# Twelve-stage transformer kernel: where PE fillers stand, how value projections are interleaved, and the order of three row gathers

## Time and profile before

| | |
|---|---|
| Three runs | 518.43, 514.8, 518.2 us |
| Median | 518.2 us |
| Profiled execution | 517.47 us, its span 515.7 us |
| PE busy | 471.1 us (91% of the span) |
| DVE busy | 330.1 us (64%) |
| ACT busy | 239.2 us (46%) |
| POOL busy | 66.7 us (13%) |
| Mean granted PE clock | 0.977 |

### The profile page before, as it was taken

How to read it: one execution, slowest core, us unless ns; L and a number is a source line. 1 busy time by engine, 2 the same in 40 slices (tenths; PEclk the granted TensorE clock), 3 DMA queues, 4 the chain that set the end, 5 groups by cost and what they waited for, 6 DMA issues and landing times.

```text
span 515.7 us, 10193 instructions
## 1 busy us (share of the span) xinstructions
PE 471.1 (91%) x4120; PEld 388.0 (75%) x4120; DVE 330.1 (64%) x815; ACT 239.2 (46%) x480; POOL 66.7 (13%) x149
## 2 busy tenths in 40 slices
PE   8988999999875869899989899889999999999897
PEld 6857885555664868656557779769899899999797
DVE  5666579984745836898335464376777777755644
ACT  7223546777400434666733246275566565532131
POOL 1220124000016020200014005500000000001000
PEclk9989999999898898999999999899999999999999
DMA  7908301910177734000019000000000000019000
GB/s 261 396 3 175 74 1 41 208 22 1 30 282 255 291 93 159 1 1 0 2 60 390 3 1 1 2 0 1 1 0 2 1 1 1 1 42 417 34 1 5
DMA packets 9070, 42.05 MB, mean 82 GB/s; under 512 B 2287, under 2 KB 4919, under 8 KB 6327
## 3 DMA queue, kind: packets, MB, share of 16 engines
q1 hardware_dynamic: 7297, 32.73, 19.5%
q0 software_dynamic: 1728, 8.68, 4.6%
HBM read 34.72 MB, written 0.08 MB: 67 GB/s over the span
## 4 chain that ended last, share of the span: by engine, by line
PE 61%; DVE 18%; DMA 7%; issue 6%; POOL 4%; ACT 3%; SPq 1%; POOLq 0%; DVEq 0%; ACTq 0%
PE banks L281 55%; PE banks L284 6%; DVE peaks L1566 4%; DMA p_const<-in_const 3%; DMA region<-in_tree_v,leaf_no 2%; DMA region<-in_tree_f,leaf_no 1%; DVE probs L1563 1%; DVE small L2559 1%; POOL mv L386 1%; DVE probs L634 1%; DVE nmax L633 1%; DVE nmax L630 1%; DVE xnT L399 1%; ACT probs L655 1%; SPq L307 1%
## 5 line engine op out<-in xcount | busy, mean ns | idle before, releaser
L281 PE MATMUL banks<-identb 128*128 128x128 bf16 x944 | 69.2, 230 | 8.4 <-DMA region<-in_tree_q,leaf_no 3.9
L281 PEld LDWEIGHTS banks<-identb 128*128 128x128 bf16 x944 | 63.3, 104 | 11.4 <-DMA region<-in_tree_q,leaf_no 4.1
L1566 DVE TENSOR_REDUCE peaks<-banks 128x1 f32<-128x1024 f32 x56 | 66.5, 1220 | 4.2 <-PE banks L281 3.1
L2559 DVE TENSOR_REDUCE small<-banks 128x1 f32<-128x1024 f32 x32 | 39.1, 1222 | 24.3 <-PE banks L281 24.1
L2653 ACT CAST weights_hi<-banks 128x512 fp32r<-128x512 f32 x64 | 35.0, 590 | 27.4 <-PE banks L284 23.4
L284 PE MATMUL banks<-p_first,probs 128*128 128x128 f32 x320 | 44.2, 275 | 3.5 <-ACT probs L658 1.7
L2644 ACT ACTIVATE probs<-banks,nmax 128x1024 f32<-128x1024 f32 x32 | 35.6, 1115 | 24.5 <-DVE nmax L2563 24.4
L2569 DVE TENSOR_TENSOR weights_lo<-banks,weights_hi 128x512 fp32r<-128x512 f32 x64 | 41.4, 683 | 7.4 <-ACT weights_hi L2653 7.4
L284 PEld LDWEIGHTS banks<-p_first,probs 128*128 128x128 f32 x320 | 36.4, 140 | 10.6 <-ACT probs L655 2.3
L1650 ACT ACTIVATE region<-banks,seen 128x512 f32<-128x512 f32 x64 | 37.9, 702 | 12.2 <-PE banks L281 12.2
L1650 ACT ACTIVATE region<-banks 128x512 f32<-128x512 f32 x64 | 33.4, 606 | 17.1 <-PE banks L281 16.7
(11 more groups left out here) (493 smaller groups left out, 907.6 us busy)
## 6 DMA issues: line engine op xcount, KB each, us to landing
region<-in_w_l2f SPq DMA_DIRECT2D x1, 4096.0 KB, 15.4
region<-in_w_l3f SPq DMA_DIRECT2D x1, 4096.0 KB, 13.5
region<-in_w_b SPq DMA_DIRECT2D x1, 3076.0 KB, 14.7
values<-in_ctx SPq DMA_DIRECT2D x2, 1024.0 KB, 7.9
region<-in_w_l0f SPq DMA_DIRECT2D x1, 2048.0 KB, 21.7
keys_l1x<-shared SPq DMA_DIRECT2D x8, 256.0 KB, 4.1
keys_l2x<-probsT SPq DMA_DIRECT2D x8, 256.0 KB, 5.1
region<-in_w_l3d SPq DMA_DIRECT2D x1, 2048.0 KB, 17.0
```

Source lines behind the costliest of these rows:

```text
L281: return nc.tensor.matmul(o, lhsT, rhs, start=start, stop=stop)
L1566: nc.vector.tensor_reduce(peaks[:, h // 4 % 2, i:i + 1], ps[:, 2 * a:2 * a + 2, :], AX.XY, ALU.max, negate=True).then_inc(VM.sem, VM.now(( ...
L2559: return nc.vector.tensor_reduce(small[:, half:half + 1], ps[:, 2 * half:2 * half + 2, :], AX.XY, ALU.max)
```

## The change

It has three parts.

1. In l1x each value projection is split into two halves of two matmuls, and the eight places between peaks are filled anew: key 0 and half of value 0 behind peak 0, then half a value behind each of peaks 1 and 2, and so on. Only the second half signals.
2. In l2x PE waits, behind peak 9, for the maximum of peak 6, and issues 22 fillers into bank 4; behind turn(0) it issues 20 more.
3. In l1f the two first-layer halves of v are gathered ahead of k's second layer; DVE makes v's hidden units ahead of k's products; the row maximum of the attention scores moves into the chain of v, ahead of its fourth step; the fillers ahead of tree q are 76 instead of 44.

```diff
-                def value(b):
-                    if b == 2:
+                def value(b, half):
+                    if b == 2 and half == 0:
                         pe.wait_ge(A.sem, A.at(("l2x", "k", 0)))
-                    if b == 3:
+                    if b == 3 and half == 0:
                         pe.wait_ge(A.sem, A.at((tag, "v", 1)))
-                    for j in range(4):
+                    for j in (2 * half, 2 * half + 1):
                         t = 4 * b + j
                         m = mm(ps[:, VALUE_BANKS[b], j * P:(j + 1) * P], ctxT[:, t * P:(t + 1) * P], w("v"))
-                    m.then_inc(T.sem, T.now((tag, "vp", b)))
+                    if half:
+                        m.then_inc(T.sem, T.now((tag, "vp", b)))
...
-                early = {0: (key, 0), 1: (value, 0), 2: (value, 1), 3: (key, 1), 4: (key, 2), 5: (value, 2), 6: (key, 3),
-                         7: (value, 3)}
+                early = (((key, 0), (value, 0, 0)), ((value, 0, 1),), ((value, 1, 0),), ((value, 1, 1), (key, 1)),
+                         ((key, 2), (value, 2, 0)), ((value, 2, 1),), ((key, 3), (value, 3, 0)), ((value, 3, 1),))
...
                 if first:
                     peak(9)
+                    pe.wait_ge(VM.sem, VM.at((tag, 3, 0)))
+                    keep(22, 4)
                 if masked:
                     pe.wait_ge(A.sem, A.at((tag, "v", 3)))
                 turn(0)
-                if not first:
+                if first:
+                    keep(20, 4)
+                else:
                     peak(9)
...
             if n == "q":
                 loaded(pe, "leaf0_q")
-                keep(44, 0)
+                keep(76, 0)
...
-        def tree_chain(dve, n, base):
+        def tree_chain(dve, n, base, between=None):
             h = units(n)
             for j in range(CHAIN):
+                if j == 3 and between is not None:
+                    between()
...
-                for n in "qk":
-                    tree_hidden(dve, n, tA[:, :])
-                    tree_products(dve, n)
+                tree_hidden(dve, "q", tA[:, :])
+                tree_products(dve, "q")
+                tree_hidden(dve, "k", tA[:, :])
                 tree_hidden(dve, "v", tA[:, :])
-                dve.wait_ge(T.sem, T.at("l1f.s"))
-                vl(dve, nc.vector.tensor_reduce(s[:, 0:1], ps[:, 0, 0:P], AX.X, ALU.max))
-                nc.vector.tensor_scalar(s[:, 1:2], s[:, 0:1], -1.0 / np.sqrt(float(P)), None,
-                                        ALU.mult).then_inc(V.sem, V.now("l1f.m"))
+                tree_products(dve, "k")
+
+                def largest():
+                    dve.wait_ge(T.sem, T.at("l1f.s"))
+                    vl(dve, nc.vector.tensor_reduce(s[:, 0:1], ps[:, 0, 0:P], AX.X, ALU.max))
+                    nc.vector.tensor_scalar(s[:, 1:2], s[:, 0:1], -1.0 / np.sqrt(float(P)), None,
+                                            ALU.mult).then_inc(V.sem, V.now("l1f.m"))
+
                 loaded(dve, "leaf2_v")
-                tree_chain(dve, "v", tree_bias("v"))
+                tree_chain(dve, "v", tree_bias("v"), largest)
...
                 tree_gather_halves(pool, "k", "l1f.paths.even", "l1f.paths")
+                tree_gather_halves(pool, "v", "l1f.paths.even", "l1f.paths")
                 tree_gather(pool, "k", (2,))
-                tree_gather_halves(pool, "v", "l1f.paths.even", "l1f.paths")
                 tree_gather(pool, "v", (2,))
```

More of the change, by code:

```diff
@@ L1489, in _ @@
                     if masked and k < 8:
-                        step, b = early[k]
-                        step(b)
+                        for step, *which in early[k]:
+                            step(*which)
                 if first:
                     peak(9)
+                    pe.wait_ge(VM.sem, VM.at((tag, 3, 0)))
+                    keep(22, 4)
                 if masked:
@@ L1736, in build, with tree_plan @@
         PRODUCTS = {"q": 2, "k": 2}
-        def tree_plan(n, func=False):
+        def tree_plan(n, func=False, first=None):
             if func:
@@ L1746, in tree_plan @@
                 V.plan(("h", n))
+            if first is not None:
+                V.plan(first)
             if n in "qk":
@@ L1959, in l1f @@
             A.plan("l1f.q")
-            tree_plan("k")
+            tree_plan("k", first=("h", "v"))
             A.plan("l1f.k")
             T.plan("l1f.s")
-            V.plan(("h", "v"), "l1f.m")
+            V.plan("l1f.m")
             A.plan(*(("u", "v", j) for j in range(CHAIN, CHAIN + 2)), "l1f.p")
```

## The result

The changed kernel takes 521.77 us in the median of six runs (521.6 to 524.51). The kernel before, run beside it, takes 516.57 (514.8 to 518.43). The ratio is 1.0113, 95% interval 1.0086 to 1.0139: slower by 4.4 to 7.2 us. Run again on another chip it took 520.33 us, ratio 1.0084 (1.0055 to 1.0113). The forecast of 522.0 us holds; its difference of +3.85 us is too small against the 5.2 us between the two medians.

A forecast was written before the change was run, and what follows sets the result against it. The prediction took a chain of waits, not PE's total busy time, to bound the kernel. Its terms +0.5 (l1x), -0.65 (l2x) and +4.0 (trees) gave +3.85, so 522.0 us from the median 518.2; 8-in-10 range 515.8 to 524.6.

The forecast's parts named there:

- Trees, the mechanism: In l1f k's second layer lands about 176.5, its products follow hidden v, PE idles, tree k delays the row maximum.
- Trees, the size: In l1f the row maximum starts at 183.15 instead of 179.13, +4.0 us; +2.85 at full clock, +4.95 at half.
- bound for half clock throughout: In l1f all of tree k at half clock: 6.1 us for its 34 matmuls, making the row maximum +4.95 us.
- L1x halves: In l1x half a value more ahead of peak 7 delays lows, turn and place(0) by +0.5 us; bounds 0 and +0.6.
- L2x fillers: In l2x fillers delay the first score +0.1 to +0.2 us, held clock gives -0.75; net -0.65, bounds -0.75 and +0.2.
- The prediction's sum from that figure: In l2x at 81 ns, 22 fillers take 1.78 us, 20 take 1.62; first score 0.6 us later, whole 522.5.
- A: Rival, not slower: k's path does not end last in l1f, tree k ends before about 178.3; 516.1 us; chance 0.2.
- B: Rival: k's second layer lands late in l1f, at 179.0, everything another 2.5 us later, 524.5 us; chance 0.13.
- C: Rival: clock falls ahead of 212 in l2x, fillers take 0.094 us each, about +2 on the forecast, 524.0; chance 0.12.
- The sum: Whole kernel: 0.5 for l1x, -0.65 for l2x and +4.0 for l1f give +3.85 us, 522.0 from the median 518.2.

The follow-up runs named there:

- the candidate: Kernel before with l2x's 22 and 20 fillers and 16 fillers ahead of the turn of l1x: 516.57 us against 516.26, ratio 1.0011.
- the run with 78: All of the trees' part alone plus 78 fillers on PE between tree q and tree k, against the kernel before: 522.54 us against 515.64, ratio 1.0128.

## Why the prediction was right, step by step

- **Trees, the mechanism**: right in its steps. The landing of k's second layer at v's old place in the bytes, the products of k behind hidden v, PE empty in between, a stretch of half clock behind the idle time, and tree k exposed in front of the maximum are all in the trace. The run with the new gathers and DVE's old order shows that the gathers' order is enough for it.
- **Trees, the size**: +4.0 forecast, +5.5 and +5.0 in the changed kernel's two profiles, +4.65 in this part's alone. I had taken one slow stretch of 3.3 us across tree k, 5.2 us in all; it took 6.31 and 6.52. Two things were mis-sized. The first is the price of a matmul at half clock, 0.18 us: the 18 matmuls in 3.30 us of the earlier trace rows count some that reach over the ends of the stretch, and from start to start it is 0.213 us. With one slow stretch tree k takes 5.69 us, as it did in the trees' part alone, with the new gathers only and in the candidate. The bound for half clock throughout was therefore too low as well: 34 of 0.213 are 7.2 us, not 6.1. The second is the length of the slow stretch, about 4.7 us of tree k and not 3.3. Of the 1.5 us missing in the first profile, 1.1 is tree k's length, 0.5 of it the price and 0.6 the longer stretch. Another 0.3 is that its first rows came 15.4 us behind DVE's first row of q (178.16 - 162.74) and not 15.1, of which hidden v's later end is 0.2.
- **L1x halves**: the 0.5 us at place(0) is measured as 0.56 and 0.63 us. The whole cost 1.9 us (0.9 to 3.1) alone, above the stated bound of 0.6. The failed assumption is that moving work on PE changes nothing but its end: the gap ahead of the turn grew from 0.78 to 1.23 us, and a stretch of half clock followed in two of three profiles with unfilled halves. It cost 0.7 and 0.95 us there; with the 0.56 at place(0) that is at most 1.5 of the 1.9 us, and the rest is open.
- **L2x fillers**: their own price was 0.16 or 0.17 us, as worked out (0.1 to 0.2), and 22 took 1.40 us in the trace, which is 64 ns each. The Trainium skill's 81 ns (TensorE: Matmul & The Clock Gate, Back-to-back issue gap) is not what this stream of one repeated identity shows. The prediction's sum from that figure was also off: 20 fillers of 1.62 us behind a turn that ends 0.35 us later would put the first score near 215.9, some 0.9 us late, not 0.6. The gain of 0.75 is real in the profile (0.77), but the kernel before does not lose it in every execution: with these fillers alone the median was 0.2 us slower (-0.6 to +1.1 us), where 0.65 faster was forecast, just outside.
- **Rivals**: A, not slower, fell at the point named for it: tree k's first input was at 178.1, where A needed its end by 178.3. B, a late landing, did not occur: 177.3 is 176.5 and the shift of 0.74 at the first row of q. C did not occur: the clock was 1.0 from 205 to 228, and the fillers took 64 ns each. Its 0.094 us for a filler at half clock has the same miscount as the matmuls above; in the run with 78, 58 of them took 6.48 us, 0.11 each.
- **The sum** of 3.85 lies just under the interval of 4.4 to 7.2 us of the first comparison and within the 2.8 to 5.8 of the second. Measured alone, the parts cost 4.7, 1.9 and 0.2 us, 6.8 together against 5.2 for the whole, which the intervals allow. So the trees were put 0.7 us too low, the halves 1.4 and the fillers 0.85. That the time came within 0.2 us is luck: the three runs known beforehand had a median 1.6 us above that of all six, and from 516.57 the same sum gives 520.4, 1.35 us too low.

## What to carry to other kernels

Where transfers share full DMA engines (their share was 1.00 to 1.04 in the earlier trace rows), putting one ahead is putting another behind. Before swapping, count what stands between each landing and the point where both are needed, and fetch first what has the longer tail. Here that was k's second layer, with its products, 4 us of matmuls and the scores behind it, against 3.9 us of v's hidden units, which the maximum needed only by DVE's order. A wait that ends last by half a microsecond is worth about half a microsecond, whatever its own length. Fillers held the clock in all profiles of the short gap of l2x, though no median shows a gain. They need to be sized to end before the awaited data; in the gap ahead of tree k, whose start moved by 2.7 us, 36 left the clock to fall and 78 stood in the way.

## What the runs showed of the hardware

- The same idle time may or may not be followed by a fall of the clock: in l2x gaps of 1.12 and 0.92 us with one small piece of work between them were followed by half clock from 216.9, and by half clock in five of the eight other profiles without fillers there. The same steps took 9.20 us at full clock and up to 11.27 us.
- A recorded matmul of 128 columns in float32 with its weight load took 0.11 us from start to start at 2.4 GHz and 0.213 at 1.2 GHz, in tree k of the changed kernel. Dividing a whole tree's time by its 34 records mixes the two (6.31 / 34 = 0.186).
- Landings of the queued gathers repeated to about 1 us when counted from DVE's first row of q. K's second layer, in the new order, was taken up by ACT 14.6 us behind it in the changed kernel's first profile, 13.7 in its second and 14.4 with the new gathers only; in the old order, by 10.5 us before and at 11.7 with DVE's order alone. V's first half, in the old order, came at 13.2 before (175.17 - 162.00) and at 13.1 with DVE's order alone (174.25 - 161.18). Which bytes stood ahead decided the order and some 3 us; the rest varied from execution to execution.
